# A tile's two weight loads move from the sync engine's queue to GpSimd's indirect transfers

## The reference, cut to what matters

```python
x = L0_attn_hidden_states                  # (4, 1024, 128)
xn = _layernorm(x)
x = x + attn(xn) + ffn(xn)
# attn: q, k, v projections, causal convolution of 4 taps, SiLU, delta rule in chunks of 32 steps
#       (a 32 x 32 triangular system per chunk and head, a state carried from chunk to chunk),
#       two FIR filters (3 and 31 taps), a gate network that mixes the four, RMS norm, W_o
# ffn:  8 experts, each token goes to the best 2 of them with softmax weights
topv, topi = jax.lax.top_k(x @ Wgate + bgate, 2)
z = (x @ W1 + b1) * (x @ W2 + b2)
g = z @ Wg + bg
y = (g * sigmoid(g) * (z @ Wl + bl)) @ W3 + b3
```

## Time and profile before

| | before |
|---|---|
| runs | 883.74, 886.43, 887.36 us; median 886.43 us |
| the profiled execution's own time | 884.17 us |
| its span, first to last instruction | 882.4 us |
| TensorE's granted clock, mean over the span | 0.842 of full speed |
| transfers | 64.92 MB, mean 74 GB/s |

### The profile page before, as it was taken

One profiled execution on the slowest core, in us unless ns is written; L12 is line 12 of the kernel. 1 busy time (PEld: TensorE's weight loads), 2 busy tenths in 40 slices (PEclk: granted clock), 3 DMA queues, 4 the chain that ended last, 5 costly groups with the idle time before them and its releaser, 6 DMA issues.

```text
span 882.4 us, 31011 instructions
## 1 busy us (share of the span) xinstructions
PE 658.0 (75%) x13276; PEld 502.2 (57%) x13276; DVE 568.8 (64%) x1233; ACT 299.6 (34%) x519; POOL 458.6 (52%) x519
## 2 busy tenths in 40 slices
PE   2434856877687878878898686978878788899772
PEld 2223845666465656566666555666566646676651
DVE  6888957536747865965577546864477748533573
ACT  2221024323343425342254334333433343334230
POOL 3730168634826754676475755387435662723323
PEclk9985567989887968997899898898889798999775
DMA  7221121323113214131332204131324311310350
GB/s 290 107 96 54 61 54 39 105 64 86 26 39 78 64 32 114 39 77 53 88 108 64 77 14 108 44 92 38 54 61 74 69 38 45 93 53 31 107 196 12
DMA packets 62488, 64.92 MB, mean 74 GB/s; under 512 B 39824, under 2 KB 47888, under 8 KB 62224
## 3 DMA queue, kind: packets, MB, share of 16 engines
q1 hardware_dynamic: 54880, 46.84, 17.8%
q0 software_dynamic: 5888, 12.07, 6.1%
q10 hardware_dynamic: 1584, 4.04, 1.2%
HBM read 45.35 MB, written 17.56 MB: 71 GB/s over the span
## 4 chain that ended last, share of the span: by engine, by line
PE 29%; issue 21%; POOL 20%; DVE 18%; DMA 6%; ACT 3%; SPq 3%; DVEq 0%; POOLq 0%; ACTq 0%
PE ps_shared L1629 5%; PE ps_shared L1850 4%; POOL y_d L1042 4%; POOL xs L1031 3%; PE ps_g L1625 3%; PE ps_l L1625 3%; PE ps_x L1625 3%; DVE acc L1392 3%; PE ps_shared L1767 3%; POOL sumsq L996 2%; SPq L881 2%; DMA system_d<-masked 2%; DVE solve_prod L1466 2%; PE ps_shared L1625 2%; POOL ssq_o L1068 2%
## 5 line engine op out<-in xcount | busy, mean ns | idle before, releaser
L1042 POOL DMA_INDIRECT y_d<-work,put_i x92 | 92.3, 1004 | 80.5 <-DVE work L1605 57.4
L1031 POOL DMA_INDIRECT xs<-xn_d,owner_i x92 | 94.7, 1030 | 60.2 <-issue 24.6
L1625 PE MATMUL ps_x<-xr,w_up 128*128 128x512 f32 x276 | 98.4, 476 | 17.9 <-issue 12.0
L1076 POOL TENSOR_TENSOR z<-work,z 128x512 fp32r<-128x512 f32 x46 | 60.4, 1314 | 59.5 <-ACT z L1246 59.3
L1625 PE MATMUL ps_g<-z,w_mid 128*128 128x512 f32 x276 | 83.2, 441 | 4.6 <-POOL z L1076 4.2
L1625 PE MATMUL ps_l<-z,w_mid 128*128 128x512 f32 x276 | 82.2, 436 | 1.7 <-issue 1.1
L1392 DVE SCALAR_TENSOR_TENSOR acc<-pre,late_sb,acc 128x512 f32<-128x512 f32 x72 | 59.9, 832 | 26.9 <-ACT acc L1139 25.6
L1625 PEld LDWEIGHTS ps_x<-xr,w_up 128*128 128x128 f32 x276 | 54.8, 218 | 36.5 <-issue 18.9
L1850 PE MATMUL ps_shared<-w_plain,work 128*128 128x128 f32 x368 | 58.2, 323 | 18.1 <-DVE work L1600 13.3
L1466 DVE TENSOR_TENSOR solve_prod<-solve_T,solve_L 128x1 f32<-128x1 f32 (+14 forms) x120 | 49.4, 412 | 28.7 <-DMA solve_L<-system_d 25.3
L1850 PEld LDWEIGHTS ps_shared<-w_plain,work 128*128 128x128 f32 x368 | 53.9, 232 | 22.6 <-issue 16.5
(11 more groups left out here) (252 smaller groups left out, 1420.7 us busy)
## 6 DMA issues: line engine op xcount, KB each, us to landing
w_split<-expert_split SPq DMA_DIRECT2D x23, 768.0 KB
w_plain<-expert_plain SPq DMA_DIRECT2D x23, 196.0 KB
xa_d<-xr SPq DMA_DIRECT2D x8, 512.0 KB, 2.6
xa<-xa_d SPq DMA_DIRECT2D x8, 512.0 KB, 4.0
system_d<-masked SPq DMA_DIRECT2D x8, 256.0 KB, 2.9
x_res<-hidden SPq DMA_DIRECT2D x8, 256.0 KB, 2.8
xs<-xn_d,owner_i POOLq DMA_INDIRECT x92
y_d<-work,put_i POOLq DMA_INDIRECT x92
```

Source lines behind the costliest of these rows:

```text
L1031: pool.indirect_dma_start(xs[par][:, c, :], None, xn_d.rearrange("w p (c d) -> (w p c) d", c=CPW), bass.IndirectOffsetOnAxis(owner_i[:, w ...
L1042: pool.indirect_dma_start(y_d, bass.IndirectOffsetOnAxis(put_i[:, w * CPW + c:w * CPW + c + 1], 0), y_sb[par][:, c * D:(c + 1) * D], None) ...
L1076: pool.tensor_tensor(low[:, :], up1[i], high[:, :].bitcast(FP), ALU.subtract).then_inc(S["z_low"], 1)
L1625: made = pe.matmul(to, weights[a], x[b], start=start and n == 0, stop=stop and n == 2)
```

## The change

`load_split` and `load_plain` are taken out of SP's program and put into POOL's, with the same waits. Each is one indirect transfer of POOL that takes partition p's row from `row_i[p, t]`; bytes, buffers and semaphores are the same. The planner's costs name POOL in place of SP and one microsecond more to landing, and the tables `PULL` and `LEAN` have other values for some twenty steps each, so that the order can differ on every engine. The sums kept in SBUF and the joint loads of result rows (`fetch`) are not touched.

```diff
-    "load_split": [[(SP_, 1.2, 6.0)]], "load_plain": [[(SP_, 1.2, 4.0)]],
+    "load_split": [[(POOL_, 1.2, 7.0)]], "load_plain": [[(POOL_, 1.2, 5.0)]],
...
-PULL = {... "choose": 400, "load_split": 150, "load_xs": -200, "load_xt": 50, "mark": 50, "masks": -200,
-        "own": 300, "products": -250, "u": -150, "u_adj": 200, "x_res": 150, ...}
+PULL = {... "load_split": 50, "load_xt": -50, "mark": 250, "masks": -150, "products": -200, "u_adj": 150, "zlow": 300, ...}
-LEAN = {... "full": 5, "inv": -35, "load_x": -15, "low": 30, "mark": -30, "v_act": 30, "w_T": 15, "y_out": -8.7, ...}
+LEAN = {... "inv": -20, "mark": -35, "v_act": 60, "w_T": -15, "y_out": -13.9, "z": -1.7, ...}
...
-                elif name == "load_split":
-                    sp.wait_ge(S["placed"], 1)
-                    if w:
-                        sp.wait_ge(S["up_low"], w)
-                        sp.wait_ge(S["mid_low"], w)
-                    row = sp.value_load(row_i[0:1, w:w + 1], min_val=0, max_val=(EXPERTS - 1) * P)
-                    sp.dma_start(w_split[:, :], expert_split[bass.ds(row, P), :]).then_inc(S["in_split"], 16)
-                elif name == "load_plain":
-                    if w < 2:
-                        sp.wait_ge(S["placed"], 1)
-                    else:
-                        sp.wait_ge(S["y_sb"], w - 1)
-                    row = sp.value_load(row_i[0:1, w:w + 1], min_val=0, max_val=(EXPERTS - 1) * P)
-                    sp.dma_start(w_plain[par][:, :], expert_plain[bass.ds(row, P), :]).then_inc(S[f"in_plain{par}"], 16)
...
+                elif name == "load_split":
+                    pool.wait_ge(S["placed"], 1)
+                    if w:
+                        pool.wait_ge(S["up_low"], w)
+                        pool.wait_ge(S["mid_low"], w)
+                    pool.indirect_dma_start(w_split[:, :], None, expert_split,
+                                            bass.IndirectOffsetOnAxis(row_i[:, w:w + 1], 0)).then_inc(S["in_split"], 16)
+                elif name == "load_plain":
+                    if w < 2:
+                        pool.wait_ge(S["placed"], 1)
+                    else:
+                        pool.wait_ge(S["y_sb"], w - 1)
+                    pool.indirect_dma_start(w_plain[par][:, :], None, expert_plain,
+                                            bass.IndirectOffsetOnAxis(row_i[:, w:w + 1], 0)).then_inc(S[f"in_plain{par}"], 16)
```

More of the change, by code:

```diff
@@ L84 @@
     "choose": [[(DVE_, 5.0)], [(ACT_, 0.5)]], "count": [[(PE_, 1.2)]], "place": [[(DVE_, 9.0)]],
-    "load_split": [[(SP_, 1.2, 6.0)]], "load_plain": [[(SP_, 1.2, 4.0)]], "split_up": [[(ACT_, 0.65)], [(POOL_, 1.4)]], "split_mid": [[(ACT_, 1.1)], [(DVE_, 1.9)]],
+    "load_split": [[(POOL_, 1.2, 7.0)]], "load_plain": [[(POOL_, 1.2, 5.0)]], "split_up": [[(ACT_, 0.65)], [(POOL_, 1.4)]], "split_mid": [[(ACT_, 1.1)], [(DVE_, 1.9)]],
     "load_xs": [[(POOL_, 5.1, 7.6)]],
@@ L111 @@
 }
[L112 to L121, removed]
@@ L122 @@
-LEAN = {"beta": -30, "beta_T": 45, "blend": 45, "combine": -15, "conv": -30, "delta_again": -40, "fetch": -10,
[L123 to L129, removed]
+PULL = {"beta_T": -200, "blend": -600, "combine": -250, "conv0": 50, "count": -200, "delta_T": 50, "delta_again": 350,
+        "down": 200, "fetch": 100, "fir": -350, "fir_l": -600, "fir_l_half": 200, "fir_s_T": -300, "fold": -250,
+        "full": 200, "fuse": -50, "fuse2": -400, "gate": 50, "gate_T": -300, "gates": 600, "give": -550, "inv": 200,
+        "k_T": -550, "ln": -150, "load_plain": 200, "load_split": 50, "load_x": -350, "load_xt": -50, "low": 250,
+        "mark": 250, "masks": -150, "mid_g": -100, "mid_l": -300, "mix_s": -100, "mix_v": -350, "normed": 100, "o": 50,
+        "out": 50, "owned": 600, "place": 100, "products": -200, "project": 250, "q_T": -350, "rank": -150, "rms": -250,
+        "solve_mul": -50, "solve_sum": -400, "split": -100, "split_mid": 550, "split_qkv": 100, "split_up": 200,
+        "store": -600, "swish": 50, "system": 400, "turn": -100, "u_adj": 150, "u_out": -450, "up2": 600, "v_T": -100,
+        "v_again": -200, "w_T": 200, "w_T_out": 350, "xn_out": 250, "y_put": -600, "z": -50, "zeros": 100, "zlow": 300}
@@ new lines @@
+LEAN = {"beta": -30, "beta_T": 45, "blend": 45, "combine": -15, "conv": -30, "delta_again": -40, "fetch": -10,
+        "fir": -5, "fir_l_T": -25, "fir_s_T": 5, "fuse": -20, "fuse2": 40, "gate_T": 35, "gates": -30, "give": 15,
+        "inv": -20, "inverse_out": 10, "k_T": 25, "ln": -40, "load_xs": -5.2, "mark": -35, "masks": -45, "mid_g": 12.1,
+        "mid_l": -5.2, "mix_s": 10, "mix_v": 30, "norm": -35, "o_T_out": -25, "owned": 10, "products": 45, "project": 5,
+        "rank": 30, "rms": -5, "solve_in": -15, "split_mid": -3.5, "state": 30, "store": 45, "sumsq": -15, "system": 25,
+        "times": 10.4, "turn": -7.7, "u_adj": 25, "up2": -3.4, "v_T": 40, "v_act": 60, "v_again": -40, "v_b": -60,
+        "w_T": -15, "w_T_out": -30, "xn_out": -5, "y_out": -13.9, "y_put": -10.4, "z": -1.7, "zlow": -15.6}
```

## The result

| | before | changed |
|---|---|---|
| runs | 883.74, 886.43, 887.36 us | 895.53, 896.16, 900.73 us |
| median | 886.43 us | 896.16 us |
| ratio, 95% interval | | 1.0125 [1.0073, 1.0177] |
| the profiled execution's own time / its span | 884.17 / 882.4 us | 900.73 / 899.0 us |
| mean granted clock | 0.842 | 0.827 |

By the ratio the changed kernel is slower by 1.25%, 11 us of 886; the medians lie 9.7 us apart. The profiled execution of the changed kernel is the slowest of its three, 4.6 us above their median, so that the difference of the two spans (16.6 us) is larger than the result.

A forecast was written before the change was run, and what follows sets the result against it. No engine is full; a chain from engine to engine bounds the kernel, POOL as near the bound as PE. Terms 20 + 0 + 3 - 5 + 0 = +18, less 4 for the plan, gave +14 us: forecast 899 us, range 880 to 914.

The forecast's parts named there:

- the main term: On POOL: a third of the new transfers' 60 us lies on the path, +20 us, bounds 0 and 60.
- POOL's time, 46 x 1.3 us: On POOL: 46 new transfers of 1.0 us plus a 0.3 us gap each, 60 us of its time.
- plus 3 for waits: In POOL's list: load_split's new waits for DVE's w_mid hold up due work behind it, +3 us, at most 19.
- the plan's share: In the planner's order: a plan knowing of the 46 loads places some better than by chance, -4 us.
- The load's own way: net 0: Release to landing: SP's 0.8 us falls away, POOL's 1.0 us replaces it, 4.3 us remains; 0, upper end +4 us.
- another order, 0: On every engine: about forty changed table values reorder steps; set at 0, with 8 us either side.
- SP set free, -5: In SP's queue: a late load and the late parts read start earlier, -5 us, bounds 0 and 9.4.
- The marks set beforehand: In the profile after: POOL 505 us busy, chain share 23% or more; SP under 3%; parts gap gone or elsewhere.
- (b): On POOL: new transfers fall into its free time, about 6 us on the path, SP's gain offsets; 887 us, chance 0.18.
- (c): In SP's list: its queue was the price, so freeing it makes the kernel faster, 877 to 879 us; chance 0.14.
- The sign for the landing as the price: At ACT: waiting far more than 51.6 us for w_split would mean the landing, not POOL's time, is the price.
- rival a: On POOL: DVE's port use holds up all 46 loads, 1.92 + 0.3 us each; about 916 us, chance 0.10.

The follow-up runs named there:

- e12: Kernel before, loads on SP, its order kept; POOL gets at the 46 places the loads' waits and 1.3 us of work behind them, no transfer: 907.7 us, 1.023.
- e4: Kernel before, loads on SP, its order kept; POOL gets at the 46 places a power instruction without waits or transfer: 963.1 us against 961.6, 1.006.
- e7: Same kernel as e4, run again on another slower chip, where the kernel before took 957.3 us: 958.93 us, 1.001.
- e10: Kernel before, its order kept, only load_plain moved to POOL: 907.82 us against 886.3, 1.024.
- e11: Kernel before, loads on SP, but SP reads the row number three times in place of once, so loads start later: 896.29 us, 1.010.
- e6: Both loads moved to POOL in the order of the kernel before, same kernel as e3, on another chip: 994.22 us against 957.3, 1.042.
- e5: The changed kernel itself, no edit, on a slower chip where the kernel before took 957.3 us: 981.97 us, 1.030.
- e1: The changed kernel with the PULL and LEAN tables of the kernel before, on a slower chip: 1002.96 us against 961.6, 1.047.
- e3: Both loads moved to POOL, otherwise the order of the kernel before, on a slower chip: 998.67 us against 961.6, 1.045.
- e2: The kernel before, loads on SP, with the changed kernel's PULL and LEAN tables, on a slower chip: 964.74 us against 961.6, 1.007.
- e9: Kernel before, its order kept, only load_split moved to POOL: 900.23 us against 886.3, 1.016.
- the third group: The runs e9, e10, e11 and e12, taken on one chip beside the kernel before, which took 886.3 us there.

## Why the prediction was right, and where it was not

The forecast was 899 us, slower with 0.67; measured were 896.16 us. (The sum came to 900; I wrote 899.) The side and the size are right, and the main term, POOL's time, holds. Two smaller terms look mis-sized in opposite directions, and that they offset each other is luck.

**POOL's time, 46 x 1.3 us.** The price of one was right: 1.05 to 1.09 us on the new lines, where I took 1.0, and 511.3 us busy where 505 was forecast. **A third of it on the path, plus 3 for waits: 23 us.** e12 adds just these two in the order of before and measured +21 us, a third of the 65 us that its pieces take. The share of like instructions in the chain was a good guide, on the chip on which it was read. In the changed kernel, with its own order, 10 of the 46 loads are on the chain: 9.7 us, or 12.7 with the gap of 0.3 us behind each, a fifth of 60. That is near the 16 us that the main term and the plan's share gave together. On the slower chips POOL had 6 to 8% of the chain in e4 and e7, and its time alone cost 1 to 6 us. The reason behind the share was only half seen, though: at the places shown of e10 and e12 the new work isn't spread at random, but comes due at the very release at which POOL's other work comes due.

**"The load's own way: net 0" has a wrong step.** I let SP's 0.8 us fall away and POOL's 1.0 take their place. The 0.8 us didn't fall away: POOL, too, starts 0.8 us after a release that it stands at. So the 1.0 us came on top, and half of the loads also start later, because POOL comes to them late. In the order of before e11 prices a lateness of 1.1 us at up to 9 us, twice my upper end of 4. What it costs in the changed kernel no run isolates: its chain has 7.9 us of weight-load landings against 8.0 before, so that there the term may well be near the 0 that I took, for another reason than mine. The Trainium skill, page "DMA: Bandwidth & Descriptors", section "Latency and other measured facts", gives a first byte after about 0.6 us from SP's way and about 1 us from POOL's, for the making up of the transfer. The trace agrees on the side, and its difference is larger, 1.0 us from start to use.

**The plan's share in the repair, -4, and another order, 0, look too small.** On the slower chip e6 and e5 show 1.2 points, 12 us, taken back directly, and e1 beside e3 that planning again with the old tables takes back nothing (1.047 against 1.045). So it is the new table values that repair; there are 21 that differ, 12 in `PULL` and 9 in `LEAN`, not the forty that I wrote. On a chip like that of the result the move of both loads in the order of before was not run. Its halves cost 1.6% and 2.4% there, together 36 us if they add up, which no run shows; the changed kernel costs 11. By what the values repair stays open. It isn't POOL's standing at the loads, which is the same in e6 and e5; ACT's shorter wait for `w_split` is the lead. That the same values on SP's kernel cost 0.3 to 0.7% (e2) says that they fit the move and are no better in themselves.

**SP set free, -5.** The early start is seen (the read of `parts` of window 4 starts 1.8 us after its source), but PE uses them only 1.3 us earlier than before, and no run isolates the worth of the whole, since every move of the loads also loads POOL. The two halves and the whole being slower, it is smaller than the price.

**The marks set beforehand.** There are 46 more DMA_INDIRECT of about 1.0 us, POOL is busy for 511.3 us where 505 was forecast, and SP has 2% of the chain, under 3%. POOL's share of the chain was to rise to 23% or more: in the changed kernel it stayed at 20%, in e9 and e10, with one load moved in the order of before, it fell to 17% and 18%, and only in e12, which moves no load, did it rise to 23%. The PE gap of 4.2 us before the `parts` of window 4 is gone; the longest such gap is now 5.0 us, before those of window 3. So one of my signs of being wrong did show, POOL at no more than 20% with that gap gone, and the time was neither that of (b) nor that of (c): the share alone doesn't tell the cases apart, for PE's share rose beside it. The sign for the landing as the price, ACT waiting far more than 51.6 us for `w_split`, didn't show: it waited 36.5. The new waits for `w_mid` are there, 49.6 us. The locked-out load (rival a) fell: the longest new transfers took 1.46 and 1.52 us, the means 1.09 and 1.05. Hidden (rival b) and faster (rival c) fell in every run that moved a load: all seven, the result among them, are slower, by 1.25 to 4.7%.

**What stays open.** On the slower chips the move costs 4.2 to 4.5%, where POOL's time alone and its waits alone cost together nothing. Lateness (e11) and time behind waits (e12) were not run there. They add up to 3.4% on the faster chip and would be the first candidates, but no run on the slower ones shows it, and the chains there speak against the second: of e3's 46 loads two are on it, with 2.1 us of a price of some 40. What a transfer from POOL does to the other transfers of its queue was not tried either.

## What to carry to other kernels

Idle time on an engine is cover only for work that may run in it. Work that waits for the same event as the due work behind it runs exactly when the idle time ends, and can take its full length out of the path, however long the engine stood before, as at the places shown of e10 and e12; over the 46 pieces of e12 it was a third. So ask of each moved step what releases it, not only how full its new engine is. A load that refills a single buffer right after its release can be late by its engine's arrival and by its making up, so price both: in e11 1.1 us on each turn cost at most 9 us in 23 turns. An engine that only starts transfers is a cheap place to stand: SP stood at these two releases for 298 us and had 3% of the chain.

## What the runs showed of the hardware that was not expected

- An indirect transfer of POOL over 128 rows takes 1.00 to 1.09 us in the mean of a group, whether a row has 512 B, 1.5 KB or 6 KB.
- The load of `w_split` starts 0.8 us after the profile's end of the DVE instruction that releases it, from SP and from POOL alike, when the engine stands at the wait. SP reads a register in these 0.8 us (two more reads take 1.1 us in e11), and POOL doesn't.
- The kernel before took 886 us where the result and the third group were taken, and 957 to 962 on two other chips. There PE's small matmuls stood longer with nothing that the profile shows to wait for. The group of 2048 of them in one and the same kernel, the changed one, first in the result, then in e5:

```profile
L1786 PE MATMUL ps_shared<-head_vs,taps 32*32 32x32 f32 x2048 | 35.0, 228 | 6.9 <-issue 6.8
```

```profile
L1786 PE MATMUL ps_shared<-head_vs,taps 32*32 32x32 f32 x2048 | 44.4, 228 | 22.0 <-issue 21.6
```

One matmul takes as long, 228 ns, yet the group is busy 9 us longer and has 15 us more idle. In the runs on those chips POOL had 6 to 13% of the chain in place of 20%, and the same change cost 3.0% in place of 1.25%: a chain, and the price read from it, belongs to the chip that it was taken on.
